# A routed feed-forward kernel on Trainium2: power step behind the products, first choice a stage earlier, opening of the block loop in another order

## The reference

```python
# layer 1, per sequence and head, q and k after elu(.) + 1
kv = kv + kt[..., :, None] * vt[..., None, :]
ksum = ksum + kt
y = einsum(qt, kv) / (einsum(qt, ksum) + 1e-6)
x = x + y @ W_proj + b_proj
# layer 2, n = layernorm(x)
routed = softmax(n @ Wr + br), kept for the top 2 of 8 experts, renormalized
h = relu(n @ W1[e] + b1[e])              # 128 -> 512
x = x + sum_e routed[e] * (h @ W2[e] + b2[e])   # 512 -> 128
```

## Time and profile before

| | us |
|---|---|
| median of 3 runs | 366.84 (365.74 to 367.57) |
| the profiled execution, whole | 367.57 |
| its span, first to last instruction | 365.8 |
| PE busy | 301.8 (83%) |
| DVE busy | 306.2 (84%) |
| POOL busy | 258.0 (71%) |
| ACT busy | 220.0 (60%) |

### The profile page before, as it was taken

How to read it: one execution, slowest core, us unless ns; L and a number is a source line. 1 busy time by engine, 2 the same in 40 slices (tenths; PEclk the granted TensorE clock), 3 DMA queues, 4 the chain that set the end, 5 groups by cost and what they waited for, 6 DMA issues and landing times.

```text
span 365.8 us, 8190 instructions
## 1 busy us (share of the span) xinstructions
PE 301.8 (83%) x2374; PEld 223.3 (61%) x2377; DVE 306.2 (84%) x622; ACT 220.0 (60%) x644; POOL 258.0 (71%) x254
## 2 busy tenths in 40 slices
PE   5789999779979999899585877999999999998200
PEld 5578755335545445545343766789999999997100
DVE  6988899998787999998897197999888888888186
ACT  2778502387788544444247864667777777775082
POOL 3749999744979999877786663777777777666400
PEclk9999999989999999999786599999999999999755
DMA  7990000000000000011111531224333333211298
GB/s 220 352 282 9 2 0 0 0 4 0 1 0 2 0 15 25 22 37 59 53 44 45 154 82 49 71 68 139 95 88 102 96 97 103 74 43 42 80 391 253
DMA packets 23957, 29.25 MB, mean 80 GB/s; under 512 B 3806, under 2 KB 18569, under 8 KB 23916
## 3 DMA queue, kind: packets, MB, share of 16 engines
q1 hardware_dynamic: 18934, 19.02, 17.9%
q0 software_dynamic: 4544, 9.38, 7.9%
q10 hardware_dynamic: 438, 0.33, 0.3%
HBM read 16.04 MB, written 12.67 MB: 79 GB/s over the span
## 4 chain that ended last, share of the span: by engine, by line
POOL 27%; PE 21%; issue 20%; DVE 19%; ACT 9%; DMA 3%; POOLq 1%; SPq 0%; DVEq 0%; ACTq 0%
POOL y_rows L568 18%; POOL x_rows L528 8%; PE ps L1272 6%; PE ps L1271 4%; DVE nd L926 4%; DVE work L915 3%; PE ps L1245 2%; ACT qk L772 2%; DVE rows L942 2%; ACT v L657 1%; ACT xs L676 1%; DVE x L1206 1%; PE ps L1247 1%; DVE st L801 1%; PE ps L1311 1%
## 5 line engine op out<-in xcount | busy, mean ns | idle before, releaser
L568 POOL DMA_INDIRECT y_rows<-kvt,yid x78 | 74.7, 958 | 29.3 <-issue 19.5
L737 ACT ACTIVATE ps<-ps,b1s 128x256 f32<-128x256 f32 x156 | 60.1, 448 | 35.2 <-PE ps L1427 35.2
L528 POOL DMA_INDIRECT x_rows<-rows,pos_i x64 | 62.4, 975 | 24.5 <-issue 18.0
L1152 DVE CAST wraw<-ps 128x1024 f16<-128x1024 f32 x39 | 47.7, 1224 | 14.0 <-ACT ps L737 11.5
L1156 DVE TENSOR_TENSOR wraw<-ps,wraw 128x1024 f16<-128x1024 f32 x39 | 47.8, 1224 | 1.3
L1425 PE MATMUL ps<-wraw,w1h 128*128 128x256 f16 x156 | 43.4, 278 | 5.7 <-DVE wraw L1156 3.5
L1444 PE MATMUL ps<-w,wraw 128*128 x312 | 45.3, 221 | 0.0
L1445 PE MATMUL ps<-w,wraw 128*128 x312 | 44.9, 221 | 0.0
L1426 PE MATMUL ps<-wraw,w1h 128*128 128x256 f16 x156 | 43.3, 277 | 0.0
L1427 PE MATMUL ps<-wraw,w1l 128*128 128x256 f16 x156 | 43.1, 277 | 0.0
L915 DVE TENSOR_TENSOR work<-ps,qk 128x1024 f32<-128x1024 f32 x32 | 38.0, 1214 | 5.7 <-PE ps L1272 5.6
(11 more groups left out here) (242 smaller groups left out, 768.1 us busy)
## 6 DMA issues: line engine op xcount, KB each, us to landing
wraw<-x_rows SPq DMA_DIRECT2D x39, 130.0 KB
qk<-y_rows SPq DMA_DIRECT2D x8, 512.0 KB, 6.4
wraw<-in_L_ffn_W_dram SPq DMA_DIRECT2D x1, 2048.0 KB, 11.5
out_dram<-x SPq DMA_DIRECT2D x8, 256.0 KB, 4.6
x<-in_L_attn_x_dram SPq DMA_DIRECT2D x3, 512.0 KB, 7.5
y_rows<-kvt,yid POOLq DMA_INDIRECT x78, 2.2
x_rows<-empty SPq DMA_DIRECT2D x9, 130.0 KB, 3.2
x_rows<-rows,pos_i POOLq DMA_INDIRECT x64, 2.4
```

What stands on the lines that cost most here:

```text
L528: nc.gpsimd.indirect_dma_start(out=x_rows, out_offset=bass.IndirectOffsetOnAxis(ap=pos_i[:, c, t:t + 1], axis=0), in_=rows[:, t, :], in_of ...
L568: nc.gpsimd.indirect_dma_start(out=y_rows, in_=ysb[:, n % YG, g], in_offset=None, out_offset=bass.IndirectOffsetOnAxis(ap=yid[:, n, g:g + ...
L737: ins = nc.scalar.activation(o, o, ACT.Relu, bias=b1s[:, bass.ds(e * HC + c, 1)])
L1152: nc.vector.tensor_copy(hh[:, n % 2], inner(n)).then_inc(hi_done, 1)
```

## The change

Five edits.

1. POOL, attention loop: for stages 2 to 12 `power_2(s - 2)` moves behind `weights_low`, `kv_products` and `token_ids` of its stage, still ahead of the scatters.
2. POOL: the scatters of the stages 12 to 15 go from 8, 9, 6, 6 to 6, 6, 7, 7; the other three of the first 40 follow behind the loop, ahead of `power_2(14)`. The number of all scatters is the same.
3. DVE, attention loop: `choose_first` of groups 0, 1 and 2 moves from the middle of stages 6, 10 and 13 (behind both multiplies) to the end of stages 5, 9 and 12 (ahead of both). For group 3 it is the same place in the queue.
4. The opening of the block loop. ACT: `norm_2(15)` ahead of `copy_turned(0)`, `copy_logits(4)` ahead of `copy_turned(2)` and `hidden(1)`. PE: the logits of units 13 and 14 ahead of the first blocks, and `ranks(4)` ahead of the loop instead of in its third turn. DVE: `split_low(15)` and the whole choice of group 4 ahead of the first block instead of between the blocks 0 to 2.
5. The parts of the second table come one turn earlier (`SPREAD` from 7 to 6; positions two turns earlier).

```diff
-    SPREAD = 7
+    SPREAD = 6
-    X_AT = {8: 2, 9: 3, 10: 3, 11: 3, 12: 8, 13: 9, 14: 6, 15: 6}
+    X_AT = {8: 2, 9: 3, 10: 3, 11: 3, 12: 6, 13: 6, 14: 7, 15: 7}
# POOL, loop over s
-                if 2 <= s < 13:
-                    power_2(s - 2)
                 for n in range(low, low + LOWS.get(s, 0)):
                     weights_low(n)
...
                 if s == 5:
                     token_ids()
+                if 2 <= s < 13:
+                    power_2(s - 2)
# ACT, ahead of the block loop
             norm_2(U - 2)
-            copy_turned(0)
             copy_x2T(U - 2)
             norm_2(U - 1)
+            copy_turned(0)
             copy_turned(1)
+            copy_x2T(U - 1)
             hidden(0)
-            copy_x2T(U - 1)
+            copy_logits(NG - 1)
+            copy_turned(2)
             hidden(1)
-            copy_turned(2)
-            copy_logits(NG - 1)
             copy_turned(3)
# DVE, loop over s
                 if s - 4 in ended_by:
-                    choose_first(ended_by[s - 4])
                     choose_second(ended_by[s - 4])
...
+                if s - 3 in ended_by:
+                    choose_first(ended_by[s - 3])
# DVE, behind the loop and in the block loop
-            choose_first(FIRST)
...
+            split_low(U - 1)
+            choose_first(NG - 1)
+            choose_second(NG - 1)
             y_rows_of(0)
             y_rows_of(1)
...
                 if n == 0:
-                    split_low(U - 1)
-                    choose_first(NG - 1)
-                if n == 1:
-                    choose_second(NG - 1)
-                if n == 2:
                     positions(NG - 1)
                     counts(1)
-                if n == 3:
+                if n == 2:
                     table_full(1)
...
-                if n == 6:
+                if n == 5:
                     table_bounds(1)
# PE, ahead of the block loop and in it
             turn_x2(U - 3)
-            turn_block(0)
             logits(U - 3)
             turn_x2(U - 2)
+            logits(U - 2)
+            turn_block(0)
             turn_block(1)
+            turn_x2(U - 1)
             up(0)
-            logits(U - 2)
-            turn_x2(U - 1)
-            up(1)
             logits(U - 1)
             turn_block(2)
+            up(1)
             turn_block(3)
+            ranks(NG - 1)
...
-                if n == 2:
-                    ranks(NG - 1)
```

More of the change, by code:

```diff
@@ L1176, in _ @@
                 if n == 0:
-                    split_low(U - 1)
-                    choose_first(NG - 1)
-                if n == 1:
-                    choose_second(NG - 1)
-                if n == 2:
                     positions(NG - 1)
                     counts(1)
-                if n == 3:
+                if n == 2:
                     table_full(1)
                     table_ends(1)
-                if n == 4:
+                if n == 3:
                     table_expert(1)
                     table_pick(1)
-                if n == 5:
+                if n == 4:
                     table_start(1)
                     table_row(1)
-                if n == 6:
+                if n == 5:
                     table_bounds(1)
```

## The result

The changed kernel takes **382.24 us** (median of 4 runs, 381.3 to 382.68), the kernel before on the same chip 367.2 us (365.74 to 367.8): a ratio of 1.0412, 95% interval 1.0375 to 1.045. The forecast of slower was right; its size, 373.2 us with a range up to 375.9, was not. The profiled execution has a span of 382.0 us against 365.8: 16.2 us more.

A forecast was written before the change was run, and what follows sets the result against it. PE bounds the block loop from about 238 us, so delay ahead of it counts in full. Roots 3.50, first choice 2.41 and opening 0.5 sum to 6.4 us: 373.2 us against a median of 366.84, range 369.3 to 375.9.

The forecast's parts named there:

- Bound: Block loop from about 238 us: PE sets the pace, not POOL; delay ahead of `up(8)` moves the end equally.
- POOL's 6.21 us: POOL's wait at 224.54, in the opening: it goes, without a gain, since POOL is not on the path.
- Roots: Attention loop, stages 4, 6 and 7: ACT's `norm_2` waits for the later root, +1.05, +1.18 and +1.27, sum 3.50 us.
- The rival of harmless roots: Attention loop: POOL runs ahead enough, so only DVE and the opening cost, 2.9 us, giving 369.7 us; chance 0.13.
- First choice: DVE, attention loop: multiplies and denominators come behind the choice; group 0 costs 0, group 1 0.89, group 2 1.52, sum 2.41 us.
- The port: Stage 7: POOL's products might hold DVE's `split_low` 3.5 us, about 0.9 on the path; taken as 0, 0.9 kept in range.
- The clock: Opening, about `up(1)` to `up(2)`: PE at 1.2 GHz behind a wait, up to 1.9 us; taken as 0, 1.9 kept in range.
- the opening: Start of the block loop: first copy 1.2 us later, `hidden(0)` to `up(8)` 0.6 to 0.7 shorter, net +0.5 us.
- The form of the sum: Whole kernel: separately costed terms added, 3.50 + 2.41 + 0.5 = 6.4 us.
- The rival "clock and port on top": Whole kernel: 1.9 us of clock and 0.9 of port added to the forecast, giving 376.0 us; chance 0.15.
- The signs that it named: Last stage's `turn_y` 6 us later, distance from there to the end the same within 1 us, among others.
- Scatters: POOL, stages 12 to 15: earlier roots end ACT's waits of 4.52 and 0.90; the former gains nothing, the latter helps the opening.

The follow-up runs named there:

- second and third profiles of the changed kernel: The changed kernel run again unaltered in two later sets, against the kernel before: 426.17 us (1.0088) and 425.47 us (1.0067).
- the third set: Later runs beside the kernel before (422.63 us): its trace run 422.05, edits 2, 4, 5 414.67, those with stage 9's products behind the scatters 412.41, changed kernel 425.47 us.

## Why the prediction was right and where it was wrong

- **Bound.** Right: PE bounds the block loop, POOL doesn't, and what is lost ahead of it reaches the end in full. POOL's 6.21 us went and gave nothing.
- **Roots.** Right: 3.38 us against 3.50, in the stages named, by waits of 0.92, 0.96 and 1.12 us, and 3.67 in the run with edit 1 alone. The rival of harmless roots is out. But each wait for the root was costed by itself; that it hands on to PE a wait of 1.93 us was not followed.
- **First choice.** Right for groups 0 and 1 (0.01 and 0.89). DVE waited 4.31, 3.74 and 4.21 us for `lg` in stages 5, 9 and 12 (105.31, 146.15, 178.65) where some 4 were forecast, and its wait for the ranks of group 0 shrank from 2.54 to 0.16 us (115.52), which is what hid that group. Group 2 was mis-sized, 2.16 instead of 1.52. Behind PE's wait of 1.65 us at 181.47 four matmuls took 3.40 us instead of 1.88, and those 1.5 us, which the term doesn't have, were partly won back in the following stages.
- **The port: the failed step.** The prediction knew the row and the rule, put the danger at stage 7 with 0.9 us, and took 0. In stage 7 nothing came of it. The hold came in stage 11, where the two engines were 2.7 us apart before: 2.8 us on DVE, and 4.17 us of the step with the clock behind it. The step asked where the products of a stage stand in the kernel before, and not by how much edit 1 brings POOL forward and edit 3 sets DVE back, at every `split_low`. The rule of the Trainium skill that the prediction quotes, "SBUF — State Buffer", section "SBUF: two separate sides", agrees with 156.81 as it did with the earlier trace rows: the operation ended with the second product. It doesn't say whether a waiting operation gets in between two products, and that differs here: in stage 8 of the changed kernel `split_low` ended at 132.53, behind the first product only, and the second, from 132.20 on, took 2.32 us instead of 2.1.

```profile
130.95 1.58 DVE L942 TENSOR_TENSOR rows<-xs,rows 128x256 f16<-128x256 f32 x1 [1.02 <-ACT rows L680]
...
130.12 4.40 POOL L499 TENSOR_TENSOR wraw<-qk,v 128x1024 f32<-128x1024 f32 x2
```

- **The clock: the other failed step.** Its one row had the right size (1.9 us behind a wait of 3.40), and the prediction applied it to the opening alone and took 0 there, "as DVE leads until `up(8)`". DVE did not: PE waited for it at 228.53 and 231.37, and in the run with the opening alone 1.9 of its 2.30 us are the clock. It also fell in stage 8 (1.7 us), stage 11 (1.4), stage 13 (1.5) and longer in stage 3.
- **The form of the sum.** It added edits that were costed one by one. Up to stage 11 the roots cost 3.67, the choice 0.93, both 10.25 us. The rival "clock and port on top" named both mechanisms, and priced each of them once: 1.9 and 0.9 us, where the clock was lower than before in five places and the hold took 2.8. That the direction came right owes nothing to luck: roots and choice alone would have given it. The signs that it named show the same: the last `y_s` came 14.33 us late where some 6 were forecast, and from there to the end it took 1.88 us more where 1 was the bound.
- **Scatters.** Edit 2 was taken at 0 and never run alone. In the ledger it lies in the stages 12 to 15 and isn't separated there.
- **Stage 3.** In every trace with edit 1 an operation of `scales()` at line 898 on DVE takes 0.94 us instead of 0.27, up to 73.91. POOL's first low part runs beside it (line 509, 72.68 to 73.84); in the kernel before that stands behind the root, which waits for ACT, and starts at 75.51: 0.67 us. The other 1.3 of the 2.00 are the clock, at 1.2 GHz up to 83.9 us instead of 79.7. In the second and third profiles of the changed kernel stage 3's `norm_2` starts at 86.88 and 86.31, not later than the 86.92 of the kernel before, so this part is one execution's.
- **Still open.** Why the clock fell in stage 8 in some executions and not in others is not settled. PE waits 1.92 to 1.94 us there in seven profiles with edit 1: in four the clock fell (all with both edits), in three it stayed (one with both, two with the roots but not the choice). Nor is it settled why `split_low` gets in between the two products in stage 8 and not in stages 9 and 11. Nor is the source of the waits without a releaser, nor why the changed kernel, 9.8 us late at stage 11 in the third set, ends only 2.8 us late there: it meets 5.2 us of such waiting at the first down copy (253.07) where the kernel before meets 18.85, and this was seen, not tried.

## What to carry to other kernels

Two edits on two engines that share something (a port, a clock, a queue) are costed together: write down for each meeting point how far apart the engines are before, and how each edit moves each of them, not forgetting what an edit takes away: a wait that kept the two in step. Here an operation of 0.4 us was free when it started 1.8 us ahead of the products, and held when it started 0.4 ahead of them or 0.3 to 1.9 behind their start; where that is near, the hold belongs in the sum. And a new wait of some 2 us on TensorE goes into the range with the matmuls behind it at half the clock (here 1.4 to 1.9 us each), each place for itself: behind the same wait it fell in about half of the profiles.

## What the runs showed of the hardware

- An operation of VectorE with two inputs in SBUF, 0.41 us long, took 3.20 and 4.90 us beside two back-to-back products on GpSimd, and 3.52 in the kernel before: it wasn't let in between the two. It started 0.41 us ahead of them in the second case. In stage 8 it took 1.58 us and did get in between.
- TensorE's clock fell to 1.2 GHz behind waits of 1.65 to 4.71 us, and once behind 0.23 us, with 0.91 shortly before; in another execution of the same program it stayed at 2.4 GHz behind 1.93 us, and in the kernel before behind 2.56 us (66.73).
- The same chip ran the same kernel in 427.04 and in 366.79 us in two sets. In the first, matmuls of the up projection stood 1.4 to 2.1 us apart in places instead of 0.11, and engines waited up to 19 us with no releaser in the trace; an order of the opening that costs 0.75% in one gained 1.5% in the other.
